# A new order for the fifteen steps of a perceiver layer, with its prologue and its weight loads rearranged

## The reference

```
x = x + xattn(layernorm(x), ctx)    # Q = x Wq; K = cos((ctx Wk) Wr + br); softmax(Q K) ctx Wv
x = x + attn(layernorm(x))          # causal top-8 of x x^T, softmax of (x Wq')(x Wk')^T over the picked ones,
                                    # message = weights @ x, gelu(mix x + (1 - mix) message) * scale
x = x + ffn(layernorm(x))           # router: 1 of 8 experts for each token, gelu(x W1[e] + b1[e]) W2[e] + b2[e]
```

## Time and profile before

| | |
|---|---|
| median of 3 runs | 447.17 us (442.69 to 450.54) |
| the profiled execution | 446.33 us, span 444.2 us, mean granted clock 0.978 |
| busy share | TensorE 93%, VectorE 56%, ScalarE 58%, GpSimd 54% |
| chain that ended last | TensorE 71%, SyncE's queue 15%, DMA 4% |
| steps 1 to 15 | about 21 to 245 us |
| expert blocks alone | from about 300 us on |

### The profile page before, as it was taken

One profiled execution on the slowest core, in us unless ns is written; L12 is line 12 of the kernel. 1 busy time (PEld: TensorE's weight loads), 2 busy tenths in 40 slices (PEclk: granted clock), 3 DMA queues, 4 the chain that ended last, 5 costly groups with the idle time before them and its releaser, 6 DMA issues.

```text
span 444.2 us, 10438 instructions
## 1 busy us (share of the span) xinstructions
PE 411.5 (93%) x3121; PEld 281.9 (63%) x3121; DVE 248.5 (56%) x808; ACT 255.9 (58%) x582; POOL 237.7 (54%) x458
## 2 busy tenths in 40 slices
PE   7977999999999999999898878889999999999991
PEld 7423445454455544545344667679999999998991
DVE  2637478878988888788788655543222222222210
ACT  1474777888888988888678745253333232424240
POOL 1760567767788788888667765451222232222210
PEclk9987999999999999999999998999999999999997
DMA  9897899896986987789999624765685656465100
GB/s 174 188 251 214 216 273 273 202 214 174 278 186 150 240 202 212 185 206 260 190 296 310 220 79 132 234 173 206 239 304 187 200 180 217 165 192 198 57 0 2
DMA packets 119450, 87.46 MB, mean 197 GB/s; under 512 B 78622, under 2 KB 109088, under 8 KB 119268
## 3 DMA queue, kind: packets, MB, share of 16 engines
q1 hardware_dynamic: 111460, 75.96, 62.7%
q0 software_dynamic: 3744, 9.46, 7.0%
q10 hardware_dynamic: 4192, 1.38, 1.7%
HBM read 79.15 MB, written 8.53 MB: 197 GB/s over the span
## 4 chain that ended last, share of the span: by engine, by line
PE 71%; SPq 15%; issue 4%; DMA 4%; DVE 2%; ACT 1%; another core or an unknown queue 1%; POOL 0%; DVEq 0%; ACTq 0%; POOLq 0%
PE pK L1513 19%; PE pT L1500 17%; SPq L575 10%; PE pK L1475 8%; PE pT L1475 7%; PE b L1420 3%; SPq L570 3%; PE b L1659 3%; PE b L1554 3%; PE b L1619 2%; PE b L1598 2%; DMA f_row<-rows_by_token,token_i 2%; DMA token_i<-tokens_by_expert 2%; SPq L563 1%; PE b L1648 1%
## 5 line engine op out<-in xcount | busy, mean ns | idle before, releaser
L1272 ACT ACTIVATE XF<-pT,b_now 128x128 f32<-128x128 f32 x184 | 52.7, 370 | 97.1 <-PE pT L1500 91.8
L1513 PE MATMUL pK<-W,XF 128*128 x368 | 86.6, 387 | 5.9 <-issue 4.1
L1500 PE MATMUL pT<-XF,stage 128*128 128x128 f32 x736 | 87.0, 275 | 0.3 <-issue 0.3
L1500 PEld LDWEIGHTS pT<-XF,stage 128*128 128x128 f32 x736 | 85.9, 192 | 2.1 <-issue 1.1
L1513 PEld LDWEIGHTS pK<-W,XF 128*128 128x128 f32 x368 | 68.8, 193 | 15.5 <-issue 6.9
L409 POOL DMA_INDIRECT f_row<-rows_by_token,token_i x23 | 23.8, 1035 | 83.3 <-DMA out_dram<-XF,token_i 70.3
L1475 PE MATMUL pK<-stage,Wkr 128*128 128x512 f32 x128 | 63.0, 618 | 0.0
L1475 PE MATMUL pT<-stage,Wkr 128*128 128x512 f32 x128 | 61.8, 606 | 1.1 <-DVE stage L726 1.1
L1247 ACT ACTIVATE stage<-stage 128x512 f32<-128x512 f32 x64 | 40.7, 637 | 12.8 <-DVE stage L787 12.6
L787 DVE TENSOR_TENSOR stage<-stage 128x512 f32<-128x512 f32 x64 | 46.2, 722 | 0.7
L726 DVE STREAM_TRANSPOSE stage<-XF 128x1024 f32<-128x1024 f32 x32 | 39.5, 1234 | 12.4 <-DMA XF<-in_ctx_dram 11.3
(11 more groups left out here) (196 smaller groups left out, 666.1 us busy)
## 6 DMA issues: line engine op xcount, KB each, us to landing
stage<-in_L_ffn_W_dram SPq DMA_DIRECT2D x23, 1024.0 KB, 5.4
stage<-in_ctx_dram SPq DMA_DIRECT2D x32, 512.0 KB, 5.4
XF<-in_ctx_dram SPq DMA_DIRECT2D x248, 64.0 KB
W<-in_L_ffn_W_dram SPq DMA_DIRECT2D x8, 1024.0 KB
rows_by_token<-rows_out SPq DMA_DIRECT2D x16, 256.5 KB
ctx_last<-in_ctx_dram SPq DMA_DIRECT2D x64, 32.0 KB, 4.5
X<-in_x_dram SPq DMA_DIRECT2D x1, 1536.0 KB, 7.8
tokens_by_expert<-no_token POOLq DMA_DIRECT2D x2, 576.0 KB, 4.2
```

The costliest lines, as they stand in the source:

```text
L1272: ins = act.activation(f_hT[b][:, n * P:(n + 1) * P], pT[i][:, (n % 4) * P:(n % 4 + 1) * P], ACT.Gelu, bias=b1_now[:, b, n:n + 1])
L1500: mm = pe.matmul(pT[i][:, (n % 4) * P:(n % 4 + 1) * P], W1[q][:, c, n * P:(n + 1) * P], f_inT[:, q % 2, c * P:(c + 1) * P], start=c == 0, ...
L1513: mm = pe.matmul(p_out, f_hT[q % 2][:, n * P:(n + 1) * P], W2[:, bass.ds(e, 1), n, :].rearrange("p o d -> p (o d)"), start=n == 0, stop=n ...
```

## The change

The same instructions are issued, in another order; nothing is computed differently.

- TensorE: the first projection of group s+1 moves from the top of step s+1 to the end of step s (ahead of value_project); the other three follow scores, xn_T and probs_T with h_T. small_scores moves from behind the last projection to right behind values, ahead of queries. message moves behind the router. rank moves behind xn_T.
- VectorE, ScalarE: new orders in the steps and in the prologue.
- GpSimd: in the steps messages moves ahead of last_value, base and mix to the end, rstd_out ahead of scatter. In step 15 gather(0) and messages(13) come last. The loads of the two scalars move here, and the mask of own tokens is built with the other masks.
- SyncE: in the prologue group 2's first half goes ahead of group 1's rows; four loads of group 1's first half, bv and Wv are issued by ScalarE; W2's loads move to steps 3, 4, 5, 7, 8, 9, 11 and 13; load_tokens(0) goes ahead of group 15's rows.

The diff, cut to its core:

```diff
@@ gpsimd
+            for k, name in enumerate(("log_mix", "log_scale")):
+                pool.dma_start(logs[:, k:k + 1], a["L0_attn_" + name].partition_broadcast(P)).then_inc(S["logs_ld"], 16)
             rstd_x(0)
...
             for s in range(1, NG):
                 if s >= 2:
                     rstd_h(s - 2)
-                    base(s - 2)
-                    normal_h(s - 2)
-                if s == 3:
-                    own_parts()
-                if s >= 3:
-                    mix(s - 3)
-                last_key(s)
-                last_value(s - 1)
...
-                if s == NG - 1:
-                    scatter(s // 2 - 3)
-                    gather(0)
...
+                if s >= 2:
+                    normal_h(s - 2)
+                last_key(s)
+                if s == 2:
+                    pool.wait_ge(S["w_ld"], 16 * W_LOADS)
+                if 2 <= s < NG - 1:
+                    messages(s - 2)
+                last_value(s - 1)
...
+                if s >= 4:
+                    rstd_out(s - 4)
+                if s >= 2:
                     base(s - 2)
+                if s >= 6 and s % 2 == 0:
+                    count_pair(s // 2 - 3)
+                    tokens_of(s // 2 - 3)
+                if s >= 7 and s % 2:
+                    scatter(s // 2 - 3, (0,) if s + 1 < NG else (0, 1))
                 if s == 3:
                     own_parts()
                 if s >= 3:
                     mix(s - 3)
...
+                if s == NG - 1:
+                    gather(0)
+                    messages(s - 2)
@@ sync
             sp.wait_ge(S["ctxT_r"], 1)
-            for j in range(2):
-                load_by_feature(1, 0, j)
+            load_by_feature(1, 0, 0)
+            load_ctx(0, 0)
+            load_last(0, 0)
             sp.wait_ge(S["ctxT_r"], 2)
             for j in range(2):
                 load_by_feature(1, 1, j)
-            load_ctx(0, 0)
-            load_last(0, 0)
-            sp.dma_start(bv[:], a["L0_xattn_bv"].partition_broadcast(P)).then_inc(S["bv_ld"], 16)
-            sp.dma_start(Wv[:], rows(a["L0_xattn_Wv"])).then_inc(S["w_ld"], 16)
-            load_ctx(1, 1)
-            load_last(1, 1)
             sp.wait_ge(S["ctxT_r"], 3)
             for j in range(2):
                 load_by_feature(2, 0, j)
+            load_ctx(1, 1)
+            load_last(1, 1)
...
+            W2_AT = (3, 4, 5, 7, 8, 9, 11, 13)
...
+                if g == NG - 1:
+                    load_tokens(0)
                 next_group(g, g % 2)
...
-                if g >= 3 and g % 2:
-                    load_w2(g // 2 - 1)
-                if g == NG - 1:
-                    load_tokens(0)
+                if g in W2_AT:
+                    load_w2(W2_AT.index(g))
...
@@ vector, the steps
+                ctx_turned(s, 1)
+                if s >= 2:
+                    residual_moments(s - 2)
+                score_max(s - 1)
+                if s >= 6 and s % 2 == 0:
+                    route(s // 2 - 3)
+                if s >= 7 and s % 2:
+                    places(s // 2 - 3)
+                    probability(s // 2 - 3)
+                if s + 1 < NG:
+                    ctx_turned(s + 1, 0)
+                if s == NG - 1:
+                    plan_experts(1)
+                whole(s, 0)
+                inverse_sumA(s - 1)
+                fraction(s, 0)
+                whole(s, 1)
+                if s >= 4:
+                    residual_out(s - 4)
+                if s >= 4:
+                    out_stats(s - 4)
+                if s >= 4:
+                    out_moments(s - 4)
+                if s >= 3:
+                    inverse_sumB(s - 3)
                 if s + 1 < NG:
                     next_stats(s + 1)
                 if s >= 2:
-                    residual_moments(s - 2)
-                ctx_turned(s, 1)
+                    small_turned(s - 2)
+                if s >= 2:
+                    masked(s - 2)
+                fraction(s, 1)
+                mean_value(s - 1)
+                if s >= 2:
+                    top(s - 2)
+                whole(s, 2)
+                if s >= 2:
+                    mark(s - 2)
                 if s >= 3:
-                    inverse_sumB(s - 3)
                     weights(s - 3)
...
@@ scalar
-            act.activation(sumA[:], ident[:, 0:1], ACT.Sin)
+            load_table(ACT.Sin, 0)
+            act.dma_start(Wq[:], rows(a["L0_xattn_Wq"])).then_inc(S["wq_ld"], 16)
...
             act.mul(Wkr[:, 1, :], pT[1][:, 0:D], INV_2PI).then_inc(S["wkr_half"], 1)
...
+            act.wait_ge(S["ctxT_r"], 1)
+            for q in range(P // T):
+                act.dma_start(*quarter_by_feature(1, 0, 1, q)).then_inc(by_feature_ld[0], 16)
...
                 turn(s, 0)
-                xnT_copy(s)
                 first_exp(s - 1)
                 if s >= 7 and s % 2:
                     router_exp(s // 2 - 3)
+                turn(s, 1)
...
+                xnT_copy(s)
                 if s >= 4:
                     gelu_y(s - 4)
-                probsT_copy(s - 1)
                 if s >= 2:
                     hT_copy(s - 2)
-                turn(s, 1)
+                probsT_copy(s - 1)
+                turn(s, 2)
                 sine(s, s % 2, 0)
-                turn(s, 2)
-                queries(s)
                 sine(s, s % 2, 1)
                 turn(s, 3)
+                queries(s)
                 oT_copy(s - 1)
@@ tensor
+            ctx_project(1, 0, 0)
 
             for s in range(1, NG):
-                ctx_project(s, 0, 0)
-                if s == 1:
-                    ctx_project(s, 0, 1)
                 scores(s - 1)
+                ctx_project(s, 0, 1)
+                xn_T(s)
                 if s >= 7 and s % 2:
                     pe.wait_ge(S["logits_r"], s - 4)
                     rank(s // 2 - 3)
-                xn_T(s)
-                if s >= 2:
-                    ctx_project(s, 0, 1)
+                ctx_project(s, 1, 0)
                 probs_T(s - 1)
                 if s >= 2:
                     h_T(s - 2)
-                ctx_project(s, 1, 0)
+                ctx_project(s, 1, 1)
                 if s >= 2:
                     similar(s - 2)
                 values(s - 1, max(0, (s - 5) // 2))
-                queries(s)
-                ctx_project(s, 1, 1)
                 if s >= 2:
                     small_scores(s - 2)
+                queries(s)
                 value_T(s - 1)
                 if s >= 4:
                     out_T(s - 4, max(0, (s - 5) // 2))
-                if s >= 3:
-                    message(s - 3)
+                if s + 1 < NG:
+                    ctx_project(s + 1, 0, 0)
                 value_project(s - 1)
                 if s >= 4:
                     router(s - 4)
+                if s >= 3:
+                    message(s - 3)
```

118 lines of the change are left out of this document (39 added, 79 removed).

## The result

The changed kernel takes 452.4 us (median of four runs, 450.06 to 453.02), the kernel before 445.75 (four runs, 442.69 to 450.54). The ratio is 1.0163, 95% interval 1.0117 to 1.0209; it leaves out the execution of 450.54, which fell in a slower state that both kernels show at times. The forecast was 446.0; the range 437 to 453 holds the time, the sign is wrong. The profiled execution has a span of 447.9 us and took 450.06, 3.7 more than the profiled one of before.

What follows compares the result with a forecast made beforehand. It took two nearly equal limits, TensorE's order and the load queue feeding VectorE's transposes. -6.5 + 5.1 + 1 - 0.5 = -0.9 gave 445.4 us, 446 as the median; range 437 to 453.

Steps and rivals of the forecast that it cites:

- The feed: SyncE's queue of context loads for VectorE's transposes limits the steps at 14.74 us a group; -5.5 us at group 14.
- the prologue's -5: Prologue: six issues fewer on SyncE (3 us) and 2 us less waiting for a transpose, 5 us by group 3.
- the -5 for SyncE's lost waits: Steps from 101.44 to 146.69 us: SyncE no longer waits for compute, about 5 us gained.
- the +4.5 for W2: Load queue ahead of group 14: eight W2 loads instead of six, 2.2 us each, 4.5 us lost.
- TensorE's saving: TensorE's steps: fewer runs of strips save 0.5 us a step, period 13.5 us, bounds 0.3 and 0.9.
- VectorE's lateness: Small transpose and mask ahead of small_scores: 0.4 us late in odd steps, on time in even ones, bounds 0 to 1.5.
- The hand-over: From scores(14) to in_T(0): gather(0) stands later on GpSimd, +5.1 us on the old 16.0, bounds +3 and +7.
- Tail: Behind in_T(0): bias1(0), the residual and block 1's token loads are done early, -0.5 us.
- -6.5: scores(14) comes 6.5 us earlier: 5.5 from the load queue and 1 from step 14.
- the clock's +1: TensorE's clock may fall after idling ahead of in_T(0): +1 us, bounds -1.9 and +3.8.
- Rival (b): Loads come no earlier, DMA engines being full: 0 at group 14, hand-over +5, 450 to 453 us; chance 0.17.
- Rival (c): small_scores waits for VectorE every step, deciding above 1.2 us late; at 2 us late 455 to 460 us; chance 0.07.

Runs made afterwards that it cites:

- e2: Kernel before with only the change's prologue, old step orders on all engines and old places of W2's and the tokens' loads: 443.02 us, ratio 1.0014 to the kernel before.
- j1: Changed kernel with queries and the next group's first projection put between values and small_scores on TensorE: 450.54 us, ratio 1.0177 to the kernel before.
- e1: Changed kernel with gather(0) in step 15 issued directly behind last_value(14) on GpSimd: 450.39 us, ratio 1.0198 to the kernel before.
- f3: Kernel before with the change's prologue and TensorE's new step order, the other engines' steps in the old order: 447.11 us, ratio 1.0105 to the kernel before.
- g4: Kernel before with the change's prologue, old step orders, and W2's eight loads in steps 7 to 14: 447.43 us, ratio 1.0046 to the kernel before.
- e3: Changed kernel loading one of the eight W2 matrices, used by every expert block (7 MB less): 449.68 us, ratio 1.0162 to the kernel before.
- g1: Changed kernel with mix on GpSimd ahead of count_pair, tokens_of and scatter: 453.64 us, ratio 1.0228 to the kernel before.
- g2: Changed kernel with mix first on GpSimd, and places and probability behind ctx_turned(s + 1, 0) on VectorE: 454.0 us, ratio 1.0215 to the kernel before.

## Why the prediction was wrong

**The feed: the step that failed.** I read SyncE's unbroken queue and 14.74 us a group as a limit, and put everything that TensorE and VectorE did behind it ("it ends in waiting for the transposes"). In the kernel after SyncE waits for VectorE, VectorE waits for a load once, and 7 MB less changed one step, the tenth, by 0.7. Term by term: the prologue's -5 was -2.7 at scores(4); the -5 for SyncE's lost waits and the +4.5 for W2, together -0.5, were +4.2 over steps 5 to 13, because the compute that was to run ahead became slower itself; the -1 of step 14 came as -1.1. The feed was the limit in single steps: step 2 of the changed kernel, step 4 of e2, step 10 of several. My own sign for it, that the feed is no limit "if TensorE never waits in steps 3 to 13", named the wrong consumer: TensorE does wait, but for VectorE's small transpose, and the wait to look for was VectorE's for its loads.

**TensorE's saving, mis-sized.** Predicted 0.5 us a step (13.5); measured 0.22 in even steps (13.73) and 0.11 in odd ones (13.88), below the lower bound of 0.3. I priced each edge of a run of strips alike. The sentence of the Trainium skill, "TensorEngine Tiling (Array Packing)", Key Properties, that a change of tiling mode drains TensorE and a change of tile doesn't, which I had weighed as the sceptical reading, lies nearer to the trace than my sum.

**VectorE's lateness, mis-sized and mis-placed.** Predicted: 0.4 in odd steps, 0 in even ones, nothing else late. Measured: 0.29 in even steps (0.98 and 1.05 in steps 10 and 14) and 0.60 to 0.65 in odd ones at small_scores, 0.18 at out_T in every step from 5 on, so periods of 14.21 and 14.70 for 13.5 and 13.9. Out of this came the real miss. I costed the lost cover at one consumer, small_scores, and named three others "nobody waits". The edits showed each of them (small_scores, o_norm, out_T, value_project, message) waiting 0.2 to 1.1 us for its input in one version or another, so that here moving one instruction only moved the wait. What the new order did was to trade 2.8 us of full-array work between values and small_scores (in the step of the earlier trace rows, from 121.60 to 124.41) for 0.1 to 0.2 us of saved edges. j1 shows both halves of it: cover back, waits gone, edges paid again. That the short cover costs nothing in steps 4 to 6 of e1 shows the other condition: VectorE's work on the pairs, which I had at 1 us and which with the wait for ranks was 2.8. What each condition is worth by itself stays open.

**Prologue: direction right, size too good.** scores(1) at 37.5, predicted 34.5; what it "really gains" by group 3 was put at 5 us and is 2.4, since step 2 took 18.5 us. Its cause in the trace is the first half of group 3's context, for which VectorE waited 6.2 us (until 46.64), and small_scores 2.1 us late behind it. That was the feed too, in the place where I had it least. With the old orders behind the same prologue step 2 took 14.84 (e2), 15.69 (f3, new on TensorE alone) and 17.18 (g4), so the new order of the other engines has a part in it that no run isolates.

**The hand-over: right mechanism, two sizes off that partly cancel.** Predicted +5.1, measured +3.7, within the bounds. The statistics ended at 9.4 us behind scores(14) for 8.9, and the gather started at 16.0 for 14.7: GpSimd's rstd_out took 2.4 for 2.1, and the two scatters with base and their issue 3.2 for 2.9. But it landed in 3.65 us, which I had bounded by 5.9. TensorE idled 5.3 us for a predicted 5.5. **Tail:** -0.5 predicted; behind in_T(0) the kernel after is 0.5 shorter with the clock's cost in it, 1.1 without. The stretch differs by more than that between executions of other kernels, so this agreement is luck.

**The sum.** -6.5 became +0.4, +5.1 became +3.7, the clock's +1 is the 0.9 by which scores took longer at 250.05 and 1.1 on the transposes behind them (3.10 for 2.02), of which 0.6 is left at in_T(1) (12.0 us behind in_T(0) for 11.4), -0.5 became -1.1: 3.7 in all. The rest of the 6.65 us between the medians is the profiled run, which was the fastest of its four. That the range holds the time is luck as well: its upper end was set by rivals. Rival (b) had the time, 450 to 453, and nearly nothing gained at group 14, by a mechanism that wasn't there (e3 took the W2 loads out and the time stayed). Rival (c) had the mechanism, small_scores waiting for VectorE in nearly every step, but with a threshold that my belief in the feed had set: without a feed at 14.7 it decides from the first tenth of a microsecond, not from 1.2.

Open: what the last 0.3 us of g1's and g2's steps hang on, and how much of e1's 2.5 us reaches the end; the intervals don't resolve either. The edit with all old orders and only a part of TensorE's regrouping that touches no cover (router and message alone) wasn't tried.

## What to carry to other kernels

On in-order engines in lockstep, work between a producer and its consumer is latency cover; before regrouping for an engine's own efficiency, write down for each consumer the distance to its producer in the old and the new order, and count every distance that shrinks. When removing a wait only makes the next one as long, stop mending single waits: several chains are critical at once; look for what they have in common. Here that was the lost cover, and undoing it took the waits away but gave back what the regrouping had saved. A queue without pauses isn't a limit until something waits for its end; ask for the consumer's wait, step by step, not for how busy the queue is.

## What was unexpected of the hardware

VectorE's instructions can take nearly twice or more of their usual time beside GpSimd's. In the step above, VectorE's subtraction at 131.97 and the rounding at 133.15 took 1.26 and 0.95 us where others of their kind take 0.69 and 0.38 to 0.42, beside GpSimd's two messages:

```profile
131.55 0.38 DVE L782 TENSOR_SCALAR stage<-stage 128x512 f32<-128x512 f32 x1
131.85 0.15 DVE L954 RECIPROCAL rsumA<-sumA 128x1 f32<-128x1 f32 x1
131.97 1.26 DVE L788 TENSOR_TENSOR stage<-stage 128x512 f32<-128x512 f32 x1
133.15 0.95 DVE L782 TENSOR_SCALAR stage<-stage 128x512 f32<-128x512 f32 x1
```

```profile
131.96 0.72 POOL L461 TENSOR_TENSOR hm<-h,gain 128x256 f32<-128x256 f32 x1
132.75 1.05 POOL L463 TENSOR_TENSOR hm<-hm,gbias 128x256 f32<-128x256 f32 x1
```

That is 1.1 us in this step and again in step 12, on VectorE's way to the small transpose and out_moments. In step 6 it was 0.5 us, and there TensorE didn't wait at small_scores (13.89 us for 14.21), so this may be what makes the 0.29 us of wait in even steps; no run isolates it, and it stands beside the cover as a cause that wasn't tested. The Trainium skill, "SBUF — State Buffer", in its section on SBUF's two separate sides, says that a VectorE operation with two inputs in SBUF and a GpSimd one that reads SBUF exclude each other for a whole instruction; the trace agrees in direction (1.26 us beside GpSimd for 0.69).

The gather of the first block's rows, always of the same size, took 7.00 us when it was issued 8.9 us behind scores(14), about 8.7 at 8.6 (e1), and 3.65 at 16.0. In these three the early ones took longer, and TensorE met it 2.5 us sooner for 7.4 us of earlier issue; what it shares the DMA engines with in those microseconds was not tried.
